# One gathered tile in 104 fetched row by row on SyncE's queue, in a three-pass GNN kernel

## The reference, cut to what matters

```
def _gine_conv(x, src, dst, e, W1, b1, W2, b2):      # twice, W00.. and W10..
    msg = jax.nn.relu(x[src] + e)                    # e: two small layers on edge_weight1
    agg = jax.ops.segment_sum(msg, dst, num_segments=x.shape[0])
    h = x + agg
    h = jax.nn.relu(h @ W1 + b1)
    return jax.nn.relu(h @ W2 + b2)
...
x = _layernorm(x + L0_gnn(x))
node_feat = _mlp(x, W_node, ...)                     # relu(h @ W + b), batch norm over all rows
edge_feat = _mlp(edge_attr_4, W_edge, ...)
message = _mlp(concatenate([x[row], x[col], edge_feat], axis=1), W_msg, ...)
agg = jax.ops.segment_sum(message, col, num_segments=N)
x = _layernorm(x + agg + node_feat)
```

## Time and profile before

| | |
|---|---|
| time, median of 3 runs | 12210.97 us (12207.96 to 12225.78) |
| the profiled execution: from its first to its last instruction | 14691.4 us, 1.203 of that median |
| POOL busy | 9148.4 us, 62% of that span (9,672 gathers) |
| PE, DVE, ACT busy | 9543.3, 7533.7, 4925.7 us |
| mean granted TensorE clock | 0.667: full to about 4.9 ms, half after |
| DMA engines busy | under 30% of each stretch but the first slice |

### The profile page before, as it was taken

The page is one execution under the profiler, slowest core; times in us unless marked ns, Lnnn a source line. Parts: engine busy times, 40 slices in busy tenths (PEclk is TensorE's granted clock), DMA queues, the critical chain, the costliest instruction groups (busy, mean ns, idle before and its releaser), DMA issues. The chain is left out here.

```text
span 14691.4 us, 164775 instructions
## 1 busy us (share of the span) xinstructions
PE 9543.3 (65%) x34164; PEld 6790.2 (46%) x34164; DVE 7533.7 (51%) x15604; ACT 4925.7 (34%) x11020; POOL 9148.4 (62%) x9725
## 2 busy tenths in 40 slices
PE   3666666666666677777777777766555555555556
PEld 2544444444444444455555555544444444444444
DVE  3433434334333444455555555556666666666666
ACT  2322222222222333333333333333333333333333
POOL 6466666666666566666666666656666666666665
PEclk9999999999999655555555555555555555555555
DMA  3111111111111211122222222211122222212122
GB/s 80 32 40 40 40 41 40 41 40 40 41 40 40 54 42 43 43 47 45 46 46 46 47 46 45 47 43 41 42 45 43 44 43 44 44 44 44 43 44 47
DMA packets 580837, 647.55 MB, mean 44 GB/s; under 512 B 411208, under 2 KB 411689, under 8 KB 579722
## 3 DMA queue, kind: packets, MB, share of 16 engines
q0 software_dynamic: 309504, 476.02, 15.5%
q1 hardware_dynamic: 219142, 139.69, 3.9%
q10 hardware_dynamic: 51712, 27.54, 0.7%
HBM read 604.68 MB, written 39.43 MB: 44 GB/s over the span
## 5 line engine op out<-in xcount | busy, mean ns | idle before, releaser
L1309 PE MATMUL ps_pre<-w_e,conv_hid 97*128 97x96 f32 x12896 | 3268.4, 433 | 2144.1 <-DVE conv_part L600 1554.4
L1309 PEld LDWEIGHTS ps_pre<-w_e,conv_hid 97*128 97x128 f32 x12896 | 2873.9, 326 | 2886.6 <-issue 2393.8
L1309 PE MATMUL ps_pre<-last_w_q,last_hid 128*128 128x96 f32 x6448 | 1627.8, 432 | 1540.8 <-issue 935.3
L1309 PEld LDWEIGHTS ps_pre<-last_w_q,last_hid 128*128 128x128 f32 x6448 | 1440.1, 327 | 1928.3 <-issue 1605.6
L264 POOL DMA_INDIRECT early_got<-in_x_rows,early_idx x1612 | 1524.3, 946 | 960.5 <-issue 439.0
L264 POOL DMA_INDIRECT early_got<-h_rows,early_idx x1612 | 1520.8, 943 | 944.2 <-issue 478.3
L264 POOL DMA_INDIRECT early_got<-p_rows,early_idx x1612 | 1520.4, 943 | 926.6 <-issue 463.3
L264 POOL DMA_INDIRECT last_got<-p_rows,early_idx x1612 | 1520.8, 943 | 905.0 <-issue 430.5
L264 POOL DMA_INDIRECT conv_got<-h_rows,early_idx x1612 | 1520.8, 943 | 884.0 <-issue 435.6
L264 POOL DMA_INDIRECT conv_got<-in_x_rows,early_idx x1612 | 1520.7, 943 | 853.1 <-issue 447.1
L582 ACT ACTIVATE conv_part<-ps_pre 128x384 bf16<-128x384 f32 x1736 | 816.0, 470 | 3676.9 <-DVE ps_pre L641 2405.4
(11 more groups left out here) (255 smaller groups left out, 10572.7 us busy)
## 6 DMA issues: line engine op xcount, KB each, us to landing
conv_row<-ea_parts SPq DMA_DIRECT2D x372, 84.5 KB
last_row<-ea_parts SPq DMA_DIRECT2D x372, 84.5 KB
early_got<-in_x_rows,early_idx POOLq DMA_INDIRECT x1612
conv_got<-in_x_rows,early_idx POOLq DMA_INDIRECT x1612
early_got<-h_rows,early_idx POOLq DMA_INDIRECT x1612
conv_got<-h_rows,early_idx POOLq DMA_INDIRECT x1612
early_got<-p_rows,early_idx POOLq DMA_INDIRECT x1612
last_got<-p_rows,early_idx POOLq DMA_INDIRECT x1612
```

Source lines behind the costliest of these rows:

```text
L1309: mm = pe.matmul(ps["pre"][q % 2][:, t * C:(t + 1) * C], hid[q % 2][0:P if last else C1, t * P:(t + 1) * P], w_q[j % U][:, c * C:(c + 1) * ...
```

## The change

One tile of each turn, tile 15 of slab 3 (the last tile of that slab's chunk 3), is left out of POOL's gathers, in all three passes. SP fetches its 128 rows instead, with one DMA of 384 B for each row. For that, SP loads the tile's 128 indices into a row of one partition, `hand_i` (one DMA for each turn, 128 elements of 4 B, issued at the end of the turn before), and reads them into registers eight at a time. The rows are issued in three pieces, behind `slab_rows` of slabs 1, 2 and 3: 48, 40 and 40 rows. Ahead of the first piece SP waits for the indices, and ahead of each for the turn before to have added that chunk (`s["add"]`). DVE waits for 16 * 128 counts of a new semaphore, `hand0`, ahead of adding chunk 3 of slab 3, beside the wait for POOL's three remaining gathers of it.

```diff
+BATCH = 8
+HAND = [(V - 1, 15, ((1, 0, 48), (2, 48, 88), (3, 88, 128)))]
+HAND_OF = {"conv0": 1, "conv1": 1, "last": 1}
...
+def hand_rows(tiles, j):
+    return [(HAND[h], h, lo, hi) for h in range(tiles) for at, lo, hi in HAND[h][2] if at == j]
...
+def pool_tiles(tiles, j, g):
+    by_hand = [t for slab, t, _ in HAND[:tiles] if slab == j]
+    return [t for t in range(*group_tiles(g)) if t not in by_hand]
...
+                def load_hand(sp, h, k):
+                    slab, t, _ = HAND[h]
+                    sp.dma_start(hand_i[h][:].rearrange("o (p i) -> o p i", i=1),
+                                 a["src_t"][bass.ds(k * V + slab, 1), :, t:t + 1],
+                                 allow_slow_non_contiguous=True).then_inc(s[f"hand_idx{h}"], 16)
+
+                def fetch_rows(sp, k, j, final):
+                    for (slab, t, _), h, lo, hi in hand_rows(HANDS, j):
+                        sp.wait_ge(s[f"hand_idx{h}"], 16 * (k + 1))
+                        sp.nop(nofuse=True)
+                        if not opening(k):
+                            sp.wait_ge(s["add"], Q * (k - 1) + NC_ * slab + t // CH + 1)
+                        sp.nop(nofuse=True)
+                        for at in range(lo, hi, BATCH):
+                            _, nodes = nc.values_load_multi_w_load_instructions(
+                                hand_i[h][0:1, at:at + BATCH], engines=(mybir.EngineType.SP,), min_val=0, max_val=NPAD - 1,
...
+                            for p, node in zip(range(at, at + BATCH), nodes):
+                                sp.dma_start(got[slab][p:p + 1, t * C:(t + 1) * C], table[bass.ds(node, 1), :]).then_inc(s[f"hand{h}"], 16)
+                        if hi == P and not final:
+                            load_hand(sp, h, k + 1)
...
+                    for h in range(HANDS):
+                        load_hand(sp, h, 0)
...
                             next_idx(k, j, final)
                             slab_rows(k, j)
+                            fetch_rows(sp, k, j, final)
...
-                                for i, t in enumerate(range(*group_tiles(g))):
+                                for i, t in enumerate(pool_tiles(HANDS, j, g)):
...
+                        for h, (slab, t, _) in enumerate(HAND[:HANDS]):
+                            if (slab, t // CH) == (j, c):
+                                v.wait_ge(s[f"hand{h}"], 16 * P * (k + 1))
```

More of the change, by code:

```diff
@@ L205, in gnn_kernel @@
         fits = sb("fits", [1, 1], I32)
+        hand_i = [sb(f"hand_i{h}", [1, P], I32) for h in range(len(HAND))]
         ident = sb("ident", [P, P])
@@ L417, in edge_pass @@
             M = C1 if last else C
+            HANDS = HAND_OF[name]
             with ExitStack() as st:
@@ L533, in load_idx @@
                     load_slab_idx(sp, idx[j], slab, s[f"idx{j}"])
+                def load_hand(sp, h, k):
[13 more added lines that the diff above has]
+                                hand_i[h][0:1, at:at + BATCH], engines=(mybir.EngineType.SP,), min_val=0, max_val=NPAD - 1,
+                                skip_runtime_bounds_check_because="src names rows of the table, and the padding its last one")
+                            for p, node in zip(range(at, at + BATCH), nodes):
+                                sp.dma_start(got[slab][p:p + 1, t * C:(t + 1) * C], table[bass.ds(node, 1), :]).then_inc(s[f"hand{h}"], 16)
+                        if hi == P and not final:
+                            load_hand(sp, h, k + 1)
                 w_hid = w_hid1 if last else w_hid0_at if stats else w_hid0
@@ L1159, in landed @@
                         for g in range(len(GROUPS)):
-                            t0, t1 = group_tiles(g)
-                            sp.wait_ge(s[f"got{j}{g}"], 16 * (t1 - t0) * k)
+                            sp.wait_ge(s[f"got{j}{g}"], 16 * len(pool_tiles(HANDS, j, g)) * k)
                             sp.nop(nofuse=True)
@@ L1393, in add_rows @@
                             if c == start:
-                                t0, t1 = group_tiles(g)
-                                v.wait_ge(s[f"got{j}{g}"], 16 * (t1 - t0) * (k + 1))
+                                v.wait_ge(s[f"got{j}{g}"], 16 * len(pool_tiles(HANDS, j, g)) * (k + 1))
+                        for h, (slab, t, _) in enumerate(HAND[:HANDS]):
+                            if (slab, t // CH) == (j, c):
+                                v.wait_ge(s[f"hand{h}"], 16 * P * (k + 1))
                         add_gathered(v, j, q, q % 2, Q * k + q)
```

## The result

The changed kernel takes 12,100.36 us, the median of 4 runs (12,098.86 to 12,103.21), against 12,211.42 (12,207.96 to 12,225.78): the ratio is 0.9909, with a 95% interval of 0.9894 to 0.9923. The forecast was 12,095.

A forecast was written before the change was run, and what follows sets the result against it. The prediction took POOL's gathers, 1.248 us each, to bound the kernel. Leaving out 93 saves 116 us, with SP's row fetches hidden: 12,211 - 116 = 12,095 us, range 12,075 to 12,300.

The forecast's parts named there:

- POOL is the bound in a timed run: POOL's gathers: 9,672 at 1.248 us each, 12,071 us, run almost without pause in a timed run.
- The sum of 12,146 us: POOL's whole span: 12,071 us of gathers plus 2.8 us before the first and 72.7 us after the last one starts.
- What POOL loses: POOL's queue: 93 gathers fewer save 116.1 us (115.4 at 1.241 us each), all on the path if POOL is the bound.
- the forecast's inner range: Whole kernel: 12,075 to 12,130 us, allowing gathers of 1.23 to 1.25 us and some saving given back at the next `close`.
- What SP gains: SP's queue: 128 row DMAs at 0.41 us and 16 register loads at 1.63, 79 us a turn, hidden under POOL's 128.5.
- Order in SP's queue, and the landing: Behind the rows in SP's queue: 48 rows take 29.5 us of a 33 us slot, leaving 16 us to land before DVE's add.
- The DMA engines: Row DMAs on the engines: at most 11 us of 128 a turn on one engine, without slowing POOL's gathers.
- Why POOL waits in the profiled execution: POOL's 2,545 us of waits: longer landings in the recorded execution hold it through gather, landing, add, product and `close`; timed runs not.
- Time is being stamped late, which a timed run need not have: SP's long instructions, such as a MOVE of 1,382 ns beside a median of 29, were taken as not real work.
- rival 1: SP becomes the bound at `fetch_rows`: 12,366 us at 0.64 us a row, 16.1 ms at 0.98; chance 0.17.
- the circle: Gather, landing, add, third part, product, `close` set the timed pace: gain 0 to a third, 12,170 to 12,211 us; chance 0.13.
- the 65 us left over in 12,211: POOL's queue: what the timed median leaves for all of POOL's waits after the 12,146 us span.

The follow-up runs named there:

- POOL's part alone: Against the kernel before, POOL skips tile 15 of slab 3 each turn and SP fills it with one DMA of 128 fixed rows: 12,119.82 us, ratio 0.9909.
- SP's part alone: Against the kernel before, SP also fetches the 128 rows into an unread tile, DVE waits for them, POOL gathers all 104 tiles: 12,234.91 us, ratio 1.0002.

## Why the prediction came out right, step by step

- **POOL is the bound in a timed run**: right, and shown. The sum of 12,146 us and some 60 us of waits is what the second profile of the kernel before shows, with 46 us of them in its three pauses; the gather is 944 ns and 1.248 us apart. Each gather left out gave 1.19 us (one a turn) and 1.21 us (four).
- **What POOL loses**: forecast 116 us, measured 111. The two profiles with gathers of 944 ns differ by 108 (12,207.1 and 12,098.9 us). There POOL's pauses of more than the ordinary 0.3 us grow from 46 to 54 us, part of it at `close` in the first turns (3.5 us at most): the little that the forecast's inner range allowed to be given back.
- **What SP gains**: the row at 0.41 us was right to the digit (0.411 us between two in one batch). The register load was mis-sized: 1.63 us forecast, 0.78 measured. The row it was taken from reads seven indices at steps of seven; the new one reads eight at steps of eight. Its own work was under-sized: 6 us a turn forecast for the first passes and 28 for the last, while the changed kernel's timeline has some 14 to 18 and 36, as the small DMAs alone were counted and not what SP does between them. Together 79 us were forecast for the rows and loads, and some 66 measured, so the sums of a turn, 85 and 107 us, came out close (80 to 84 and 102) by two errors against each other.
- **Order in SP's queue, and the landing**: right on the chip of the result, where nobody waits for a row. The run with all rows late showed, on the slower kind, that the deadline is real.
- **The DMA engines**: right. Gathers keep their 944 ns beside 11,904 single-row DMAs; single ones of 1,000 to 1,126 ns occur, but as much (up to 1,131) without the rows, in the second profile of the kernel before. A row is two packets on SP's queue, as the sum had it: the queue has 37,200 packets more than before, 400 a turn. The one DMA of 128 rows in the run with POOL's part alone is 144 packets; if the index DMA of 128 elements is as many, 256 are left, two for each row. The estimate of 256 us a turn from the Trainium skill's page "DMA: Bandwidth & Descriptors" (section "Anatomy of one DMA — SWDGE (gpsimd) path", some 2.0 us fixed for a DMA) doesn't come about: 48 rows go out in 24 us and nobody waits for them, so such fixed parts don't follow one another here. The views give no landing time of a row; that of the index DMA on the same queue is 2.2 us.
- **Why POOL waits in the profiled execution**: wrong. I put its fifth more down to the profile, and the stamps of 2 and 1,382 ns to late stamping. The second profile of the kernel before has neither, and a timed run on the other chips is as slow as the profile was. Those stalls are real time on those chips. The step that failed is "Time is being stamped late, which a timed run need not have"; on such a chip rival 1 is what happens, at 8%. Its upper price, 16,100 us, is near the 16,079 measured only in total: it had 152 us a turn for rows and loads, where the turn shown has 126. The forecast that the span would grow to some 18 ms while the timed runs don't was wrong too: span and time go together on either chip (12,098.9 and 12,100.84; 16,075.0 and 16,076.96). Nor do DVE's 2.6 ms of waits speak for the circle (1,413 us of them are put down to "remote" in the earlier trace rows, not to a landing): on the result's chip DVE waits 2,789 us for the gathers and POOL isn't held up. So why the kernel before takes 14,700 to 14,900 us on the slower kind stays open.
- So the forecast held because the timed runs and the profile were of two kinds of chip and the sum was made against the timed ones. The reading that saved it was the 65 us left over in 12,211, not the explanation of the lumps. That the result came from a chip of the faster kind was luck: on the one of the slower kind where the changed kernel ran it was 8% slower than the kernel before, and "slower" had a chance of 0.20.

## What to carry to other kernels

Multiply the steadiest instruction of an engine by its count and compare with the timed median, not with the profile's span: here 12,071 of 12,211 us named the bound that busy shares of 62 to 65% hid. Where span and median differ by a fifth, take the profile again before explaining the difference. And work moved to an idle queue should be priced for the worst chip it will meet: one tile in 104 gave 0.9% on one kind of chip and cost 8% on another, where its 64 us became 126.

## What the runs showed of the hardware

- Two kinds of chip, 22% apart on the same kernel (12,209 and 14,867 us). On the slower kind SP's instructions take irregularly some 0.7 to 1.4 us, whatever they do (a MOVE up to 1,421 ns, a row DMA once 2,087, beside 38 and 296 at most in the changed kernel on the faster kind), but a gather's 944 ns on POOL is the same. What makes the kinds differ wasn't found; one chip was of the faster kind in the experiments and four of the slower.
- An indirect gather of 64 rows costs POOL 907 ns, one of 128 rows 947 in the same run.
- Register loads of eight indices at steps of eight take 0.78 us (median, 0.53 to 1.03), of seven at steps of seven 1.64 (1.10 to 1.82), a single one 0.49 (on the slower kind). Whether the step makes the difference wasn't tried alone.
- The gather's length moves a little from run to run, by line 944 or 947 ns (minimum 940 or 943), on one chip and in one set of runs. Over 9,672 gathers 2 to 3 ns are 19 to 29 us, the size of the 23 us between the 12,208.94 us of the kernel before and the 12,231.62 of its other runs beside it, of which no profile is shown:

```profile
L264 POOL DMA_INDIRECT early_got<-in_x_rows,early_idx x1612: 940/944/2746, 2.6 to 3964.9; - x180
```
```profile
L279 POOL DMA_INDIRECT early_got<-in_x_rows,early_idx x1612: 943/947/2352, 2.8 to 3975.4; - x180
```

The first is the kernel before at 12,207.1 us, the second the one with SP's part alone at 12,234.6.
